# Attention kernel: where the next head's weights are split, and when the query scale is taken

## What is computed

```python
q = rope(rmsnorm(x @ Wq), pos); k = rope(rmsnorm(x @ Wk), pos); v = x @ Wv
k_all = concat([k_cache[pages], k]); v_all = concat([v_cache[pages], v])      # 512 + 128 keys
probs = softmax(where(valid, q @ k_all.T * SCALE, -1e30))
x = x + (probs @ v_all) @ Wo
```

## Time and profile before

| | |
|---|---|
| median of three runs | 1287.37 us (1286.99 to 1288.35) |
| the profiled execution's own time | 1285.65 us |
| its span, first to last instruction | 1283.8 us |
| granted clock of PE | full in all slices |
| busy: PE, DVE, ACT, POOL | 99%, 79%, 65%, 73% |
| chain that ended last | PE 85%, DVE 4%, DMA 3%, POOL 3%, ACT 2% |

### The profile page before, as it was taken

The page is one execution under the profiler, slowest core; times in us unless marked ns, Lnnn a source line. Parts: engine busy times, 40 slices in busy tenths (PEclk is TensorE's granted clock), DMA queues, the critical chain, the costliest instruction groups (busy, mean ns, idle before and its releaser), DMA issues.

```text
span 1283.8 us, 25202 instructions
## 1 busy us (share of the span) xinstructions
PE 1267.1 (99%) x7068; PEld 1108.1 (86%) x7068; DVE 1017.0 (79%) x2064; ACT 839.9 (65%) x2217; POOL 931.4 (73%) x1171
## 2 busy tenths in 40 slices
PE   9999999999999999999999999999999999999999
PEld 8887888888888888888888888888888888888887
DVE  6988788888888878888888888888888887658546
ACT  7676676767677667666676767676766675535444
POOL 7889988878887888888888888887887823323211
PEclk9999999999999999999999999999999999999999
DMA  6798789868976897689669957996765354363532
GB/s 219 238 269 266 215 232 265 235 180 237 269 218 171 247 274 197 181 261 269 167 193 285 275 148 209 272 260 171 205 162 170 128 190 153 110 220 121 192 120 82
DMA packets 259899, 265.66 MB, mean 207 GB/s; under 512 B 139776, under 2 KB 211072, under 8 KB 249088
## 3 DMA queue, kind: packets, MB, share of 16 engines
q1 hardware_dynamic: 253920, 228.24, 62.0%
q0 software_dynamic: 5920, 36.70, 8.5%
HBM read 182.57 MB, written 82.31 MB: 206 GB/s over the span
## 4 chain that ended last, share of the span: by engine, by line
PE 85%; DVE 4%; DMA 3%; POOL 3%; ACT 2%; issue 2%; SPq 1%; DVEq 0%; POOLq 0%; ACTq 0%
PE ps L65 26%; PE ps L66 25%; PE ps L67 25%; PE ps L1378 5%; DVE at_pT_lo L1041 1%; DMA at_qT_raw<-q_rows 1%; PE ps L2333 1%; PE ps L1420 1%; DMA shared<-in_kT_cache,at_page_idx 1%; DVE at_probs L1093 1%; SPq L420 1%; POOL at_probs L635 1%; DVE xres L1110 0%; DMA turned_rows<-at_turned 0%; ACT at_pT_hi L776 0%
## 5 line engine op out<-in xcount | busy, mean ns | idle before, releaser
L635 POOL TENSOR_SCALAR at_probs<-at_probs,at_row_inv 128x640 f32<-128x640 f32 x256 | 218.6, 865 | 94.8 <-DVE at_row_inv L1103 91.6
L829 ACT ACTIVATE at_probs<-at_probs,at_neg_max 128x640 f32<-128x640 f32 x256 | 210.1, 822 | 117.3 <-DVE at_neg_max L1093 117.2
L1093 DVE CUSTOM_DVE_ANT_0 at_probs<-ps,at_mask,at_inv_rms 128x640 f32<-128x640 f32 x256 | 223.7, 881 | 18.5 <-PE ps L67 15.1
L65 PE MATMUL ps<-ds_hi,x_hi 128*128 128x512 f32 (+1 forms) x564 | 192.8, 342 | 0.9 <-DVE x_lo L1639 0.4
L67 PE MATMUL ps<-ds_hi,x_lo 128*128 128x512 f32 (+1 forms) x564 | 192.1, 341 | 0.0
L65 PE MATMUL ps<-at_kT_hi,ds_lo 128*128 128x320 f32 x512 | 159.7, 312 | 3.4 <-DVE at_pT_lo L1041 1.6
L776 ACT ACTIVATE at_pT_hi<-ps 128x512 fp32r<-128x512 f32 x196 | 111.3, 603 | 74.9 <-PE ps L1378 71.6
L67 PE MATMUL ps<-at_kT_hi,ds_lo 128*128 128x320 f32 x512 | 158.1, 309 | 0.0
L66 PE MATMUL ps<-at_kT_lo,ds_lo 128*128 128x320 f32 x512 | 158.1, 309 | 0.0
L1041 DVE TENSOR_TENSOR at_pT_lo<-ps,at_pT_hi 128x512 fp32r<-128x512 f32 x196 | 128.7, 684 | 22.6 <-ACT at_pT_hi L776 22.5
L65 PE MATMUL ps<-at_pT_hi,at_v_hi 128*128 128x512 f32 x320 | 127.2, 398 | 3.4 <-DVE xres L1110 3.1
(11 more groups left out here) (227 smaller groups left out, 3616.6 us busy)
## 6 DMA issues: line engine op xcount, KB each, us to landing
turned_rows<-at_turned SPq DMA_DIRECT2D x62, 512.0 KB
at_pT_raw<-turned_rows SPq DMA_DIRECT2D x248, 128.0 KB
kT_pages<-shared SPq DMA_DIRECT2D x16, 1024.0 KB, 5.6
q_rows<-at_q_turned_rows SPq DMA_DIRECT2D x248, 64.0 KB
at_qT_raw<-q_rows SPq DMA_DIRECT2D x62, 256.0 KB
kv_raw<-kT_pages SPq DMA_DIRECT2D x60, 256.0 KB, 3.9
v_pages<-shared SPq DMA_DIRECT2D x14, 1024.0 KB, 5.7
kv_raw<-v_pages SPq DMA_DIRECT2D x54, 256.0 KB, 3.4
```

Of the source, the lines that this page charges most:

```text
L65: pe.matmul(out, l_hi, r_hi, start=first, stop=False)
L635: pool.tensor_scalar(probs[:, h, :], probs[:, h, :], row_inv[:, h:h + 1], 1.0, ALU.mult, ALU.mult).then_inc(probs_done, 1)
L829: act.activation(probs[:, h, :], probs[:, h, :], ACT.Exp, bias=neg_max[:, h:h + 1], scale=-1.0, accum_out=row_sum[:, h:h + 1]).then_inc(ex ...
L1093: dve.tensor_tensor_reduce(out=probs[:, h, :], in0=slot(h), in1=mask[:, b, :], scale=inv_rms[b % 2][:, h:h + 1], scalar=3.0e38, op0=ALU.ad ...
```

## The change

In round 5 of heads 0 to 6: on GpSimd the low part of the first half of the key and value weights moves from the head of the round to behind cached_values; query_scale moves behind rotate_k. On ScalarE both high parts of these weights move behind cached_values and queries. On VectorE the low parts of query parts 0, 1 and 2 move: the first from ahead of spread_queries to behind the fourth mask, the second from ahead of the fourth mask to behind inverse 2, the third from ahead of inverse 2 to behind inverse 3. No instruction is added or dropped. Rounds 5 of head 7 stay as they were.

```diff
@@ GpSimd, group() @@
-                    if b == B - 3 and not last:
-                        qkv_group(g + 1, DC)
                     if started:
                         if not keys_by_row(g1, b1):
                             cached_keys(g1, b1)
...
                     if b == B - 3 and not last:
+                        qkv_group(g + 1, DC)
                         qkv_group(g + 1, DC + 1)
                         wq_group(g + 1, 3)
...
-                    before_ending = last and b == B - 3
+                    late_scale = not started or b == B - 3
                     normalise(g1, b1, 0)
-                    if started and not before_ending:
+                    if not late_scale:
                         query_scale(g2, b2)
                     for h in range(1, G):
                         normalise(g1, b1, h)
                     if started:
                         rotate_k(g2, b2)
-                    if before_ending or not started:
+                    if late_scale:
                         query_scale(g2, b2)
@@ ScalarE, group() @@
+                    if started:
+                        cached_values(g1, b1)
+                    queries(g1, b1)
                     if b == B - 3 and not last:
                         qkv_group(g + 1, DC)
                         qkv_group(g + 1, DC + 1)
-                    if started:
-                        cached_values(g1, b1)
-                    queries(g1, b1)
@@ VectorE, group() @@
-                    if b == B - 3 and not last:
-                        qkv_group(g + 1, 0)
                     if started:
                         spread_queries(g2, b2)
                         add_y(*preceding(g, b), last and b > 0)
...
+                    mask_and_max(g1, b1, 3)
                     if b == B - 3 and not last:
-                        qkv_group(g + 1, 1)
-                    mask_and_max(g1, b1, 3)
+                        qkv_group(g + 1, 0)
                     if by_moves(g, b):
                         probs_T(g, b, 3)
                         probs_T(g, b, 4)
...
+                    inverse(g1, b1, 2)
                     if b == B - 3 and not last:
-                        qkv_group(g + 1, 2)
-                    inverse(g1, b1, 2)
+                        qkv_group(g + 1, 1)
...
                     inverse(g1, b1, 3)
+                    if b == B - 3 and not last:
+                        qkv_group(g + 1, 2)
```

## The result

The changed kernel took 1290.08 us (median of 17 runs) beside 1286.99 for the kernel before on the same chip: a ratio of 1.0022, 95% interval 1.0015 to 1.0030. It is in the range and 1.5 us above the forecast. By the ratio it is 2.8 us above the kernel before, by the medians 3.1, close to the 2.6 us that the prediction took as the least that a measurement tells. One of the changed kernel's 17 runs took 2560.07 us; it is left out of the ratio. Its profiled execution took 1287.86 us for a span of 1285.2; before it was 1285.65 for 1283.8. The change's lines lie one lower after line 676: L1377 is the L1378 of before, L1040 the L1041, L1109 the L1110.

A forecast was written before the change was run, and what follows sets the result against it. TensorE bounds the kernel, busy 1267.1 of 1283.8 us. Heads 1 to 6 give -0.8 and head 0 +2.0, together +1.2: span 1285.0, median 1288.6 us, range 1284.3 to 1291.5.

The forecast's parts named there:

- The front of round 5: Heads 1 to 6: without ds_lo ahead, the xres adder starts at 4.38 and the 0.70 us lost per round is gone.
- The turns after the fourth mask: Round 5: DVE low parts and GpSimd normalises alternate at SBUF, making the second probabilities late; 0.47 us lost per round.
- Rival (a): After round 5's fourth mask: turns cost nothing, DVE and GpSimd run side by side; 1283.5 us, chance 0.12.
- Rival (b): After round 5's fourth mask: third normalise also waits for low part 2, all later by 0.3; 1291.2 us, chance 0.26.
- The price in round 6: Heads 1 to 6: cached_keys 0.45 into round 6, adder at 5.05, so PE loses about 0.10 us.
- the limit of 4.98: In a round, the xres adder may start as late as 4.98 us without PE losing time.
- the 0.11 of the first product: PE's first product after a wait takes 0.50 us instead of 0.39, so 0.11 is added to a loss.
- rival (c): Heads 1 to 6: stall only moves from round 5 into 6, within 0.05 each; 1289.4 us, sharing my case's 0.62.
- my case: Whole kernel: turns take back most of the gain, head 0 loses; 1288.6 us, own range 1287.0 to 1290.0, chance 0.62.
- Head 0: Rounds 5 and 6: work moved behind the queries' transfer and turns cost +0.35, +0.67 and +0.9; +2.0 us together.
- as the prediction had feared: Sign of being wrong altogether: transfers of turned rows or queries land later, as queries' rows are stored over 1 us earlier.
- The order of the turns: Round 5: forecast followed the earlier trace, not the skill's first-issued order, which would lose 0.55 for 0.47, +0.5 us over six.

The follow-up runs named there:

- e3: Kernel before with only VectorE's three low parts of the query weights moved as in the change; 1285.48 us, ratio 0.9987.
- e1: The change with query_scale put back between the first and second normalise in rounds 5 of heads 0 to 6; 1284.65 us, ratio 0.9981.
- e7: The change with low part 0 of heads 1 to 6 taken over 4 of its 512 columns; 1287.93 us, ratio 1.0001.
- e2: Kernel before with only query_scale moved behind rotate_k in rounds 5 of heads 0 to 6; 1292.93 us, ratio 1.0047.
- e9: The change in heads 1 to 6 only, query_scale in its old place there, head 0 wholly as before; 1283.10 us, ratio 0.9962.
- e4: e1 with head 0's ScalarE and GpSimd order as in the kernel before, VectorE's low parts still moved; 1283.44 us, ratio 0.9974.
- e10: The kernel of e4 run again in another lot; 1282.92 us, ratio 0.9965 to the kernel before.
- e6: The change in head 0 only, heads 1 to 6 as in the kernel before; 1289.52 us, ratio 1.0014.
- e8: The whole change run again in another lot; 1290.50 us, ratio 1.0022 to the kernel before.
- e5: The change in heads 1 to 6 only, head 0 wholly as in the kernel before; 1287.87 us, ratio 0.9997.

## Why the prediction was right, and where it was not

**The front of round 5: right.** The adder starts at 4.38 (predicted 4.38), PE does not wait there, and the 0.70 is gone. e3 shows which part GpSimd has in it: without its reordering the adder is at 5.15.

**The turns after the fourth mask: right, to 0.1 us.** From 487.35, with the prediction in brackets: low part 0 ends at 10.23 (10.30), the pair at 11.95 (12.04), PE begins the second group at 12.01, low part 1 ends at 12.62 (12.72), low part 2 at 13.83 (13.80), the fourth normalise at 14.50 (14.40), query_scale at 16.30 (16.2). The loss in round 5 is 15.71 - 15.28 = 0.43 (0.47). That turns are the cause, and no transfer, is shown by e1, where the same low parts stand in the same places and the pair took 1.28, and by heads 3 and 5 of e7, which lost the wait with low part 0. In the changed kernel DVE waited for the high parts of the pair in none of the six heads. Rival (a), turns that cost nothing, falls with them. Rival (b) falls for this kernel: in all six heads low part 2 waited for the third normalise (1.22 us in head 3), not the other way round. But what it describes does happen elsewhere: in head 4 of e7 the third normalise took 1.63 us and ended behind low part 2, and that head's round 6 was 15.70.

**The price in round 6: the step that failed.** I took 0.10 and it was 0.31. The mechanism and the limit of 4.98 hold wherever the adder was late in rounds 5 and 6 and nothing else was: such a round lasts 15.28, plus what the adder is over 4.98, plus the 0.11 of the first product.

| kernel, head, round | adder | 15.28 + (adder - 4.98) + 0.11 | measured |
|---|---|---|---|
| the change, 3, 6 | 5.18 | 15.59 | 15.59 |
| e2_scale_alone, 3, 6 | 5.02 | 15.43 | 15.43 |
| e3_dve_alone, 3, 5 | 5.15 | 15.56 | 15.56 |
| e7_narrow_low0, 3, 6 | 5.02 | 15.43 | 15.43 |
| the change, 0, 6 | 6.01 | 16.42 | 16.43 |

What was mis-sized was the adder's start, 5.05 for 5.18, and 0.07 + 0.11 = 0.18 was then taken as 0.10 between the ends "with the 0.11 or without it". The 0.13 has two parts, to 0.01: round 5 ended 0.04 sooner than I had it, which puts the same query_scale later in round 6, and GpSimd's own queue was 0.10 later. So the six heads give +0.04 each and not -0.13 (the one round 5 of 15.96 is head 5's, where GpSimd came out of round 4 late: its first normalise started at 9.11 and not 8.89, and all that follows is 0.22 later; with it the six are +0.45 us together). This is rival (c): the stall moves from round 5 into round 6. Its time, 1289.4, is the nearest of all to the measured one, and I had it inside my case. The measured 1290.08 lies just above my case's own range (1287.0 to 1290.0); it is in the stated range because that took in most of (b), whose mechanism did not occur. That part is luck.

**Head 0: right in kind, the total hidden by a transfer.** Predicted +1.0 in round 5 and +0.9 in round 6; the profiled execution shows +0.06 and +1.16. Round 6 was 0.26 dearer, mostly since cached_keys came at 1.41 and not 1.2. Round 5 hangs on the landing of the queries, which changes from execution to execution. Taken from the end of ACT's wait, it is nearly a constant of the kernel as long as that landing is what ends last:

| kernel | wait ends, into round 5 | round 5 | difference |
|---|---|---|---|
| before | 3.59 | 18.47 | 14.88 |
| e9 (head 0 as before) | 3.34 | 18.23 | 14.89 |
| e3, e4, e10 (DVE moved) | 3.45, 4.29, 3.67 | 17.92, 18.73, 18.11 | 14.47, 14.44, 14.44 |
| e1 (all moved, query_scale not) | 3.22 | 18.77 | 15.55 |
| the change, e6, e7, e8 | 2.52, 3.95, 4.67, 3.57 | 18.53, 19.96, 20.66, 19.57 | 16.01, 16.01, 15.99, 16.00 |

Not in the table are e2 (15.85 at 2.72, the only run of its kind) and e5, whose head 0 is that of before and which has 16.02 (18.10 at 2.08). The landing was so early there that another path ended last: e5's chain of waits comes from GpSimd's normalises and goes through DVE's turning and low part 0, which took 1.75 us beside the rotation of the queries, and not through the transfer.

```profile
116.23 0.75 DVE at_turned L1133
...
121.50 1.17 DVE ds_lo L1046
```

At an equal landing that ends last, the change costs 1.12 in round 5 (1.02 predicted): moving DVE's low part gives 0.44 (0.69 predicted), the high and low parts that fall behind the wait cost 1.11 (1.04), and the late query_scale 0.45 (0.67). The landing came 1.07 earlier in the profiled execution of the change than in that of before, and hid it. How much the order of before would have gained from so early a landing is not shown: at 2.08, e5 had 18.10, which is 0.43 less than the change's 18.53. The early landing is no gift of the change: over its four executions it comes at 2.52 to 4.67, with the order of before at 3.59, 3.34 and 2.08. Seven executions cannot tell whether the change makes it later on the whole, as the prediction had feared.

**The sum.** By these: head 0 +1.12 + 1.16, the six heads +0.45, together +2.7 us, where I had +1.2. The medians differ by 3.1 and in e8 by 3.2. The remaining 0.4 us is not explained; it is below what the intervals can tell, and the 1.12 stands for landings that end last.

**The order of the turns, by the Trainium skill.** The Trainium skill, SBUF — State Buffer, "Who interferes with whom", lets the one that issued first have the ports. Head 4 of e7 agrees: the pair issued behind the second normalise waited for it, 1.68 for 1.28. So does e2, 1.87 for 1.28. The changed kernel does not. Its first normalise ended at 496.24 + 0.80 = 497.04, and the second was pending from then on; DVE's pair was issued at 497.50, yet the pair's first low part ran ahead of it: the two normalises ended together at 498.77, which is 0.60 behind the end of that low part (497.58 + 0.60 = 498.18). As in the earlier trace rows, the normalise was passed over once and ran behind two of DVE's instructions. The measurement decides; why it is passed over is open. Nor is the order fixed: see e1 in the last section.

## What to carry to other kernels

Work moved off a congested place must be costed where it lands, and also by what it uncovers behind it: here the low parts were free to move, and only the small instructions between two normalises made their new place nearly harmless, since these took the turns that cost 0.06 us at most. Before moving such a filler, ask what its absence lets two large instructions do to each other. Where a step waits for a transfer that scatters, compare times from the end of that wait rather than from the round's opening, and check in the chain that the wait ended last: two executions of head 0's round 5 differed by 0.06 us and hid a cost of up to 1.1.

## What the runs showed of the hardware that was not expected

In e1 the two small GpSimd instructions with two inputs ran beside DVE's low parts, L600 in 0.63 us and L602 in 1.34, and the pair lost nothing (1.28). A normalise with one SBUF input, pending when DVE goes from one low part to the next, can be passed over (2.53 us for two of 0.80 each). Whether it is passed over is not fixed by the program: in e1 the second normalise starts at 11.70 into round 5 of head 2 and at 11.71 of head 3, beside the same low parts. In heads 2, 5 and 6 it took 1.06 us and low part 2 waited, in heads 1, 3 and 4 it waited for low part 2 and took 1.64. The three normalises of heads 2 and 3, on POOL's timeline:

```profile
376.74 3.04 POOL L635 TENSOR_SCALAR at_probs<-at_probs,at_row_inv 128x640 f32<-128x640 f32 x3
...
499.29 3.20 POOL L635 TENSOR_SCALAR at_probs<-at_probs,at_row_inv 128x640 f32<-128x640 f32 x3
```

The rounds 6 of 15.33 and 15.34 follow the three heads with 1.64. And a small DVE instruction waits as a large one does: in e7 the low part of 4 columns, issued at 499.40, ended at 499.69 with the first normalise (498.88 + 0.80).

TensorE's granted clock fell inside an execution. Stretches of 5 us (busy time of each engine, granted clock, DMA share, GB/s) in head 7: e3_dve_alone has a clock of 0.71 where the kernel before has 1.00. In the 5 us ahead of it e3's PE was busy for 4.40. The first fence is e3, the second the kernel before.

```profile
985.00:990.00 5.00, 4.40 (x24) 3.18 (x22) 4.07 (x11) 4.27 (x11) 3.74 (x4) 1.00 0.43 157
990.00:995.00 5.00, 3.82 (x14) 2.78 (x13) 3.76 (x8) 3.81 (x8) 4.92 (x8) 0.71 0.29 114
```
```profile
990.00:995.00 5.00, 3.43 (x21) 2.45 (x20) 4.06 (x10) 4.75 (x13) 4.22 (x8) 1.00 0.26 107
```

In e3's chain the pieces of PE took 0.43 us there, the lower level of 1.2 GHz, and 0.23 to 0.25 from 995.61 on; ahead of them the chain had been off PE since 984.46.

```profile
984.46 0.02 issue
984.48 0.38 DVE at_probs L1093
...
991.91 0.30 PE ps L1354
992.22 0.41 PE ps L65
...
995.18 0.43 PE ps L66
995.61 0.25 PE ps L67
995.86 0.23 PE ps L65
```

Eight matmul pieces of the chain at 0.2 us more are 1.6 us, half of what the change costs. Six of e3's 12 runs show a mean clock below 1; their median is 1286.61 us, that of the other six 1284.02. In the lot of e5 to e8 the kernel before and the change have such runs too (12 of 35, and 7 of 12 for e8_whole), and at full clock alone their medians are 1286.41 and 1289.43, 3.0 us apart, so the clock does not explain the change's cost.
